# Four attention blocks on one core: the last block's key mask inside the key tile, its exps one PSUM bank at a time, another order of the merged stretch, and each bf16 term of its queries loaded behind its own store

## The reference

```python
def _L3_xattn_ref(x, mask, kv, kv_mask, Wq, bq, Wk, bk, Wv, bv):
    q = jnp.einsum('oc,bct->bot', Wq, x) + bq[None, :, None]
    k = jnp.einsum('oc,bct->bot', Wk, kv) + bk[None, :, None]
    v = jnp.einsum('oc,bct->bot', Wv, kv) + bv[None, :, None]
    ...
    attn = jnp.einsum('bhqd,bhdk->bhqk', q * scale, k)
    attn = jnp.where(kv_mask[:, :, None, :], attn, -jnp.inf)
    attn = jax.nn.softmax(attn, axis=-1)
    mean = jnp.einsum('bhqk,bhkd->bhqd', attn, v)
    ex2 = jnp.einsum('bhqk,bhkd->bhqd', attn, v * v)
    std = jnp.sqrt(jax.nn.relu(ex2 - mean * mean))
    ...
    out = (xn * std + mean) * mask.astype(x.dtype)
```

## Time and profile before

| | us |
|---|---|
| median of 3 runs | 1008.47 (1007.87 to 1010.12) |
| the profiled execution, its own time | 1012.25 |
| its span, first to last instruction | 1010.5 |
| PE busy | 935.5 (93%) |
| DVE busy | 559.5 (55%) |
| ACT busy | 456.2 (45%) |
| POOL busy | 292.4 (29%) |

### The profile page before, as it was taken

The page is one execution under the profiler, slowest core; times in us unless marked ns, Lnnn a source line. Parts: engine busy times, 40 slices in busy tenths (PEclk is TensorE's granted clock), DMA queues, the critical chain, the costliest instruction groups (busy, mean ns, idle before and its releaser), DMA issues.

```text
span 1010.5 us, 21161 instructions
## 1 busy us (share of the span) xinstructions
PE 935.5 (93%) x8450; PEld 596.5 (59%) x8450; DVE 559.5 (55%) x890; ACT 456.2 (45%) x795; POOL 292.4 (29%) x402
## 2 busy tenths in 40 slices
PE   6989989999999998999999999999999999898995
PEld 5555764666647665567646666466665675455552
DVE  4344467445664557555675456644576546664554
ACT  2423444445444544445544454345544454442424
POOL 5230222334212432115322242124321243222401
PEclk9999999999999999999999999999999999999999
DMA  9500324113140132303241130401414031310220
GB/s 362 190 38 2 125 75 146 38 43 136 36 156 19 57 139 81 108 6 126 79 146 38 43 134 32 154 28 43 141 50 143 14 120 44 119 53 2 98 55 6
DMA packets 36728, 86.54 MB, mean 86 GB/s; under 512 B 8472, under 2 KB 26008, under 8 KB 28824
## 3 DMA queue, kind: packets, MB, share of 16 engines
q1 hardware_dynamic: 36632, 85.18, 24.5%
HBM read 77.24 MB, written 7.86 MB: 84 GB/s over the span
## 4 chain that ended last, share of the span: by engine, by line
PE 67%; DVE 12%; issue 6%; DMA 5%; ACT 5%; SPq 4%; POOL 1%; DVEq 0%; ACTq 0%; POOLq 0%
PE GP L1107 6%; PE GP L1118 6%; PE GP L660 6%; DVE nm L1592 5%; PE GP L662 5%; PE PV L821 4%; PE GP L1091 4%; PE PV L860 3%; PE GP L900 3%; PE SC L883 3%; PE PV L1031 3%; DMA Qx<-q_parts 2%; PE GP L667 2%; PE SC L1018 2%; PE SC L804 2%
## 5 line engine op out<-in xcount | busy, mean ns | idle before, releaser
L1592 DVE TENSOR_REDUCE nm<-MX 128x4 bf16<-128x1024 f32 (+1 forms) x168 | 206.4, 1229 | 125.3 <-PE MX L751 48.3
L1363 ACT ACTIVATE Pr<-SC 128x1024 f32<-128x1024 f32 x120 | 122.7, 1023 | 153.6 <-PE SC L883 76.9
L1966 POOL TENSOR_TENSOR Psum<-Pr 128x512 f32<-128x512 f32 x64 | 81.5, 1274 | 163.4 <-ACT Pr L1363 163.4
L660 PE MATMUL GP<-zP,W 128*128 128x128 f32 x512 | 106.3, 290 | 7.7 <-DMA W<-w 7.7
L662 PE MATMUL GP<-uP,W 128*128 128x128 f32 x512 | 99.7, 277 | 0.0
L660 PEld LDWEIGHTS GP<-zP,W 128*128 128x128 f32 x512 | 78.3, 193 | 29.0 <-issue 27.3
L1392 ACT ACTIVATE Pr<-SC,bcol 128x512 f32<-128x512 f32 x96 | 60.8, 685 | 51.3 <-PE SC L1018 50.7
L1934 POOL TENSOR_TENSOR stat<-stat,half 128x1 f32<-128x1 f32 x24 | 13.7, 570 | 224.4 <-DVE stat L1800 171.2
L662 PEld LDWEIGHTS GP<-uP,W 128*128 128x128 f32 x512 | 78.5, 194 | 0.0
L821 PE MATMUL PV<-Pr,V 128*64 128x256 f32 x512 | 70.8, 398 | 0.0
L1118 PE MATMUL GP<-WB,work 128*128 128x256 f32 x256 | 60.8, 386 | 6.5 <-DVE work L1731 6.4
(11 more groups left out here) (221 smaller groups left out, 1750.3 us busy)
## 6 DMA issues: line engine op xcount, KB each, us to landing
W<-w SPq DMA_DIRECT2D x20, 1024.0 KB, 5.3
WA<-w1a SPq DMA_DIRECT2D x8, 1024.0 KB, 7.2
WB<-w1b SPq DMA_DIRECT2D x8, 1024.0 KB, 9.5
WA<-w2a SPq DMA_DIRECT2D x8, 1024.0 KB, 4.8
WB<-w2b SPq DMA_DIRECT2D x8, 1024.0 KB, 7.0
Kx<-k_parts SPq DMA_DIRECT2D x24, 192.0 KB
Qx<-q_parts SPq DMA_DIRECT2D x24, 192.0 KB
scratch<-U SPq DMA_DIRECT2D x14, 256.0 KB, 2.0
```

Of the source, the lines that this page charges most:

```text
L660: pe.matmul(dst, W0[:, piece, 2 * s, at:at + P], zP[:, s * P:s * P + P], start=True, stop=False)
L1363: act.activation(Pr[:, n % 4:n % 4 + 2, :], SCP[:], ACT.Exp, scale=8.0 ** -0.5 if L else 0.125)\
L1592: dve.tensor_reduce(dst, MXP[:].rearrange("p i (a k) -> p i a k", a=a), AX_X, ALU.max, negate=True)\
L1966: pool.tensor_tensor(Psum[:, c % 4, :].rearrange("p (a l) -> p a l", l=D), two[:, :, 0:D], two[:, :, D:2 * D], ALU.add)\
```

## The change

Four things. (1) The 128 mask matmuls (line 725) go. Each query block now carries a 1 in a row that no channel uses, and the mask row is added to the same row of `K3b`, by two DVE instructions per entry behind the third norm (`scalar_tensor_tensor`, 128 x 256). For this `Q3b` needs eight variants instead of four: DVE makes two, ACT six (all eight for the last entry); four lie in `Q3c`, a part of `work`. (2) Stage 3's exps go one bank at a time in every stretch. (3) `BOTH` has another order. (4) Each query term is stored and loaded by itself: the load of the high term stands right behind its store, ahead of the stores of the other two (not for the last entry), and waits for that store alone; its source repeats one term three times, as the keys' did, and the keys' loads take the form that the queries' had.

```diff
-        (0, 4, [(0, 3, 2), ("rest", 0)], [(3, 0, 0)]),
-        (0, 5, [("den", 1), ("terms", 0), (0, 3, "T"), ("recip", 0, 0)], [(3, 0, 2)]),
-        (0, 6, [], [("recip", 0, 1), (3, 1, 0)]), (0, 7, [(3, 0, "T"), (3, 1, 2)], [("den", 2), (3, 2, 0)]),
-        (3, 0, [], [(3, 2, 2), ("den", 3), (3, 1, "T")]), (3, 1, [(0, 0, "B")], [(3, 2, "T")]),
...
+        (0, 4, [("rest", 0), (0, 3, 2)], [("terms", 0)]), (0, 5, [(0, 3, "T")], [(3, 0, 0), ("den", 1)]),
+        (0, 6, [("recip", 0, 0), (3, 0, 2)], [("recip", 0, 1), (3, 1, 0), (3, 0, "T")]),
+        (0, 7, [(3, 1, 2)], [("den", 2), (0, 0, "B"), ("den", 3)]),
+        (3, 0, [("recip", 1, 0), (3, 2, 0), (3, 1, "T")], []), (3, 1, [(3, 2, 2)], []),
...
@@ key_terms, query_terms
-                store_terms(b, k_parts, (s_K3h, s_K3m, s_K3l), st_k)
+                store_terms(b, k_parts, ((0, s_K3h, st_k), (1, s_K3m, st_k), (2, s_K3l, st_k)))
...
-                    sp.dma_start(Kx[24 * j:24 * j + 24], k_parts[j:j + 1].to_broadcast([3, 8, NH * D]))\
-                        .then_inc(ld_kx, 16)
+                    sp.dma_start(Kx[24 * j:24 * j + 24], k_parts).then_inc(ld_kx, 16)
...
-                store_terms(b, q_parts, (s_Q3h, s_Q3m, s_Q3l), st_q)
-                sp.wait_ge(st_q, 48 * b + 48)
-                for j in range(3):
-                    sp.dma_start(Qx[24 * j:24 * j + 24], q_parts).then_inc(ld_qx, 16)
+                store_terms(b, q_parts, ((0, s_Q3h, st_q[0]),))
+                if not is_last(b):
+                    load_term(b, 0)
+                store_terms(b, q_parts, ((1, s_Q3m, st_q[1]), (2, s_Q3l, st_q[2])))
+                for i in range(3 if is_last(b) else 2):
+                    load_term(b, i if is_last(b) else i + 1)
+            def load_term(b, i):
+                sp.wait_ge(st_q[i], 16 * b + 16)
+                sp.dma_start(Qx[24 * i:24 * i + 24], q_parts[i:i + 1].to_broadcast([3, 8, NH * D])).then_inc(ld_qx, 16)
@@ maxima_pair3
-                    t = 2 * (g // 2) + u // 2
+                    v = 4 * (g // 2) + u + g % 2
...
-                    for i in range(2):
-                        half = slice(64 * i, 64 * i + 64)
-                        pe.matmul(M[i][:].rearrange("p (a k) -> p a k", k=D), sel[half, 0, :],
-                                  mrow[half, :].unsqueeze(1).to_broadcast([64, 2, D]), start=True, stop=False,
-                                  skip_group_check=True)
@@ scalar, mixed
-                    if is_last(b):
-                        exps_last(b, k)
+                    if L == 3:
+                        exps3(b, k)
...
-                    if b >= 0 and L == 0 and k == 4:
-                        queries3(b)
+                    if b >= 0 and L == 0 and k in (4, 5):
+                        queries3(b, (1, 3, 4) if k == 4 else (6, 5, 7))
@@ vector, behind layer_norm(b, xa, ..., 3)
+                dve.wait_ge(s_msk, N_MSK * b + 3)
+                dve.wait_ge(s_K3v, b + 1)
+                for e in range(2):
+                    ins = dve.scalar_tensor_tensor(out=K3b[:, e, :], in0=b3row[:], scalar=hmask[:, 14 + e:15 + e],
+                                                   in1=K3b[:, e, :], op0=ALU.mult, op1=ALU.add)
+                ins.then_inc(s_K3b, 1)
```

More of the change, by code:

```diff
@@ L249, in build @@
         Q3b = sb("Q3b", [P, 4, D], BF16)
+        Q3c = work[:, 1536:2048].bitcast(BF16).rearrange("p (v l) -> p v l", l=D)
         V0 = sb("V0", [P, 2, 1024])
@@ L331, in build @@
         ld_w0v = sem("ld_w0v")
-        st_k, st_q, ld_kx, ld_qx = sem("st_k"), sem("st_q"), sem("ld_kx"), sem("ld_qx")
+        st_k, ld_kx, ld_qx = sem("st_k"), sem("ld_kx"), sem("ld_qx")
+        st_q = [sem(f"st_q{i}") for i in range(3)]
         const_x = sem("const_x")
@@ L511, in shifts, with query3 @@
             return (s_T3, 4 * b + g + 1) if L == 3 else (nmT_ready, SHIFTS.index((b, L, g)) + 1)
+        def query3(v):
+            return Q3b[:, v, :] if v < 4 else Q3c[:, v - 4, :]
         def turned3(b, g):
@@ L581, in load_values, with store_terms @@
                 sp.dma_start(W0[:, 4], w0[4 + n % 2]).then_inc(ld_w0v, 16)
-            def store_terms(b, scr, ready, stored):
-                for i, s in enumerate(ready):
+            def load_term(b, i):
+                sp.wait_ge(st_q[i], 16 * b + 16)
+                sp.dma_start(Qx[24 * i:24 * i + 24], q_parts[i:i + 1].to_broadcast([3, 8, NH * D])).then_inc(ld_qx, 16)
+            def store_terms(b, scr, terms):
+                for i, s, stored in terms:
                     sp.wait_ge(s, b + 1)
@@ L683, in ready_group @@
                         pe.wait_ge(s_Q3b, b + 1)
[L684 to L685 removed]
+                    else:
+                        pe.wait_ge(s_Q3, 3 * b + g)
                     if g == 0:
@@ L730, in maxima_pair3 @@
                             half = slice(64 * i, 64 * i + 64)
-                            mm = pe.matmul(M[i][:, s * D:s * D + D], Q3b[half, t, s * P:s * P + P],
-                                           K3b[half, g % 2, :], start=False, stop=True, skip_group_check=True)
+                            mm = pe.matmul(M[i][:, s * D:s * D + D], query3(v)[half, s * P:s * P + P],
+                                           K3b[half, g % 2, :], start=True, stop=True, skip_group_check=True)
                             if s == 1:
@@ L1329, in highs3, with queries3, exps3 @@
                 act.activation(parts[:, 0, :], g[:, 0:D], ACT.Identity, bias=col("bq")).then_inc(s_Q3h, 1)
-            def queries3(b):
+            def queries3(b, which):
                 g = take(order_of(b), "q3")
                 act.wait_ge(s_Q3r, b + 1)
[L1335 to L1338, removed]
+                for v in which:
+                    ins = act.activation(query3(v), g[:, 0:D], ACT.Identity, scale=hmask[:, 4 + v:5 + v],
+                                         bias=col("bqm", v))
+                    if v == 2:
                         ins.then_inc(s_Q3b, 1)
-                ins.then_inc(s_Q3, 1)
-            def exps_last(b, k):
+                    elif v in (3, 6, 7):
+                        ins.then_inc(s_Q3, 1)
+            def exps3(b, k):
                 for j in range(2):
@@ L1354, in mixed @@
                     n = SC_AT[b + (L == 0), L, 2 * k]
-                    if is_last(b):
-                        exps_last(b, k)
+                    if L == 3:
+                        exps3(b, k)
                         if k == 4:
                             sums(b, 0)
+                        if k == 1 and b < B - 1:
+                            evacuate(b + 1, 3)
                         continue
@@ L1496, in keys3 @@
                     for e in range(2):
-                        ins = act.activation(K3b[:, e, :], g[:, 0:D], ACT.Identity, scale=hmask[:, 8 + e:9 + e],
+                        ins = act.activation(K3b[:, e, :], g[:, 0:D], ACT.Identity, scale=hmask[:, 12 + e:13 + e],
                                              bias=col("bkm", e))
-                    ins.then_inc(s_K3b, 1)
-                    wait(act, st_q, 48 * b)
+                    ins.then_inc(s_K3v, 1)
+                    wait(act, st_q[0], 16 * b)
                     act.activation(parts[:, 0, :], g[:, 0:D], ACT.Identity, bias=col("bk")).then_inc(s_K3h, 1)
@@ L1851, in body @@
                     dve.wait_ge(s_Q3h, b + 1)
-                    for t in range(2):
-                        ins = dve.tensor_scalar(Q3b[:, t, :], g[:, 0:D], col("bq"), hmask[:, 4 + t:5 + t],
-                                                ALU.add, ALU.mult)
+                    for v in (0, 2):
+                        ins = dve.tensor_scalar(query3(v), g[:, 0:D], hmask[:, 4 + v:5 + v], col("bqm", v),
+                                                ALU.mult, ALU.add)
                     ins.then_inc(s_Q3b, 1)
@@ L1972, in keys3 @@
                 pool.wait_ge(s_K3r, b + 1)
+                for stored in st_q[1:]:
+                    wait(pool, stored, 16 * b)
                 pool.tensor_copy(parts[:, 1, :], rest_k).then_inc(s_K3m, 1)
@@ L2096 @@
             at = slice(32 * r + 8 * t, 32 * r + 8 * t + 8)
-            bqm[t, at], bkm[r % 2, at] = bq[at], bk[at]
+            bqm[2 * t + r % 2, at], bkm[r % 2, at] = bq[at], bk[at]
+            if t < 2:
+                bqm[[v for v in range(8) if v % 2 != r % 2 and (v < 2) == t], 32 * r + 8 * t] = 1.0
     w0 = np.stack([a["L0_xattn_" + n].T for n in ("Wqkv0", "Winj0", "Wqkv1", "Winj1")], axis=1)
```

35 lines of the change are left out of this document (16 added, 19 removed), and 2 rows, old and new, of the table TAKEN.

## The result

The changed kernel takes 1052.3 us (median of 4 runs, 1049.23 to 1055.08) against 1008.9; the ratio is 1.0429 [1.039, 1.0468]. It is slower by 4.3%, outside the range forecast. The profiled execution took 1049.23 us, its span is 1047.4.

The account below looks back on a forecast made before the run. PE was taken as the bound (busy 93% of the span), DVE nearly as full in the first part. Stretches -8.4, queries' loads -2.5, last stretch +1.4: -9.5 us, giving a median of 999.0; range 986 to 1009.

Parts of the forecast that it names:

- The first part: From q3 to first scores3 in a merged stretch: DVE sets the pace, scores3 starts at 14.7 us, against 14.6 undisturbed before.
- The masks of the first part thus buy no time there: From q3 to first scores3: -0.2 us of PE work is given back as +0.3 of waits for DVE.
- The second part: From first scores3 to the projections: 17.3 us for 18.6; with the first part -1.2 a stretch, -8.4 in seven.
- The exps' -0.3 a stretch: Second part: two one-bank exps free the first bank half a microsecond sooner than a two-bank exp, -0.3 us per stretch.
- The queries' loads: Loads of the query terms ahead of scores3: all landed at 14.1 us from q3, 0.6 to spare before 14.7.
- one load of 196.6 KB in the new form takes 2.55 us: One query term's load on three DMA engines at 77 GB/s, the rate seen while the keys load in the repeating form.
- The last stretch: Three loads behind all stores land at 12.5 us, scores3 was at 10.7: +1.8, less 0.4 of masks, +1.4 us.
- The K3b instructions: Two DVE instructions of 0.48 us per entry behind the third norm: hidden in DVE's idle time; uncovered, 7.6 us.
- Rival (d): Three engines too few for the queries' loads: data end at 6.3 + 3d; d 3.6 gives +13 us, 1021.5; chance 0.12.
- The rule by which the forecast was to be judged wrong: PE's wait for the queries' load over the earlier 6.0 us by more than 2 would mean three engines bind.
- These rows don't show what delayed it there: The queries' load before the change, late in four of seven stretches by up to 1.7 us: cause left open.
- I take back -2.5: PE's waits for the queries' load outside the last stretch: 2.5 of 4.4 us regained, 0 to -4.8 kept possible.

Follow-up runs that it names:

- a_old_loads: The changed kernel with the queries' and keys' loads as before (all terms onto 24 rows, three times, behind all three stores): 993.82 us, ratio 0.986 to the kernel before.
- i_turned: The changed kernel with the repetition turned: each of a term's 8 rows repeated three times in place, slowest dimension 8, not 3; keys laid out to match: 993.49 us.
- g: The changed kernel with the high term's load behind all three stores, still repeating, weights issued behind the loads without waiting for them: 1055.34 us, ratio 1.0439 to before.
- c: The changed kernel, but SP waits until the queries' terms have landed before it issues the next entry's weights: 1028.04 us, ratio 1.0185 to the kernel before.
- h: The changed kernel with the high term's load behind all stores, and the weights issued only when the queries' terms have landed: 1014.4 us, ratio 1.0025 to before.
- p_masks: The kernel before with only the mask row in K3b and eight query variants (old order, exps and loads): 1003.14 us, ratio 0.9936 to the kernel before.
- f: The changed kernel with each term's load cut into three of eight rows, written three partitions apart, keys laid out to match: 996.97 us, ratio 0.9863 to before.

## Why the prediction was wrong

Forecast 999.0 us, measured 1052.3: 53 us off, on the other side of no change.

- **The first part** was right where the queries are there: PE was ready at 14.5 in the change and started at 14.44 in a_old_loads, for 14.7. Its reason was wrong in part. "The masks of the first part thus buy no time there" is refuted: they buy 0.8 to 0.9 us (14.58 to 13.64, 15.24 to 14.44), and the order costs 0.7 to 0.8.
- **The second part**: 17.3 forecast, 17.0 measured without the new loads. A stretch gains 14.58 + 18.6 - 31.44 = 1.74 us for the forecast 1.2; seven give -12.2 for -8.4. The exps' -0.3 a stretch was -0.2.
- **The queries' loads** are the step that failed: "Landed at **14.1**", where in the third stretch they landed at 20.4 and scores3 started at 20.7. The number of engines was right: the DMA share of 0.21 while the loads run alone is that of three. The Trainium skill (DMA: Bandwidth & Descriptors, "Why a DMA increments its semaphore by 16 and not by 1") has the slowest dimension set it; the trace agrees, also in i_turned, where 8 in that place doubles the share to 0.43 and mends the kernel. Sizes were wrong. First, "one load of 196.6 KB in the new form takes 2.55 us" was taken from a window without other traffic; beside the weights a packet takes 0.6 us, so the 16 packets that each engine carries for loads 1 and 2 need 9.6 us and not 5.1. Second, the first packets of a load take longer than the 0.31 us of the others, mostly 0.7 to 1.5 in the change's merged stretches; the sum had none of that. Third, the stores behind the high term's load were seen at 9.0, not 7.5. Moving them ahead is worth nothing while the weights move up with them (g), and 13.6 us when they don't (c to h). In the third stretch the data of loads 1 and 2 start at 10.5 for the forecast 8.9, and from there to the landing it is 9.9 us for 5.2; that is the whole 6.3 us from 14.1 to 20.4.
- **The clock** was in no term: after waits of 4.4 to 6.3 us TensorE ran at 1.2 GHz for a while, 13.1 us in all. Such a piece also followed the two longest waits in the merged stretches before the change, of 1.6 and 1.8 us; the second part took 19.8 there behind the first of them, for 18.6. None followed the waits of 1.7 to 2.6 in p_masks.
- **The last stretch**: 12.5 forecast, 13.76 measured. By the trace's packets the data start at 5.0 and end at 13.1, for the forecast 4.8 and 12.5, nearly all at 0.31 us a packet since no weights flow here; the other 0.6 us lie between the last packet and scores3.
- **The K3b instructions**: hidden, as forecast; 84.9 us stand between the stretches in all kernels.
- **Rival (d)** is what happened, by its own mechanism ("when stores and weights share these engines"), at a chance of 0.12 and a price too low: it took 3.6 us for a load beside the weights. By the packets of the third stretch that is what the high term's load took, ahead of the weights, and loads 1 and 2 took nearly 5 each. Its formula needs a d of 4.7 to give 6.3 + 14.1 = 20.4; that value is fitted, not found. The rule by which the forecast was to be judged wrong, over 2 us more of this wait, showed it: 43.8 for 6.0.
- **"These rows don't show what delayed it there"**, of the late load before: its third store. In the third stretch it was issued at 6.5 and landed 3.3 us later, for the 2.0 of the others (what held it isn't shown); issued at 5.1, as the new order has it, its loads were in time in all seven stretches of a_old_loads. "I take back -2.5" was worth -4.4.

The row set against the keys' window was no quiet one either. The window "while the queries load", 0.87 and 195 GB/s, ends at 520.05, and SP had issued the next entry's weights at 516.51. So that is the rate of the queries' loads with weights among them. In the last stretch, where no weights follow, the plain form alone moved 140 GB/s (the issue of the weights, then the window of the last stretch):

```profile
516.51 0.36 SPq L529 DMA_DIRECT2D WA<-w1a  x1
...
981.80:985.30 3.50, 3.09 (x22) 1.32 (x22) 3.06 (x3) 0.00 (x0) 0.00 (x0) 1.00 0.62 140
```

A load beside the weights was thus to be seen in the trace before the change; the sum took its rate from the keys' window, which has none.

Put together by the profiled spans: -12.2 in seven stretches, -4.4 of old waits, -1.7 in second parts that were longer than 18.6 before, -0.5 in the last stretch are -18.8, for 992.0 - 1010.5 = -18.5; the new loads add 55.4.

What stays open: why the first packets of a load take so long, and so differently (0.3 to 1.6 us); what it is in neighbouring rows that slows a load; and why all engines slow down when one of these loads runs beside the weights. i_turned changes the number of engines and the rows written at a time together; no run keeps three engines and changes the rows. None of these was tried further.

## What to carry to other kernels

A load's form decides how many DMA engines carry it. Before one that somebody waits for is moved earlier, ask what flows on the same engines by then, and price it from a window with that traffic, not from a quiet one. If a source must repeat, put the repetition inside, behind a dimension that gives more engines, and let one load reach partitions that lie apart. And a wait of several us on PE can cost more than its length, when what follows runs at the lower clock.

## What the runs showed of the hardware

- **The queries' loads and the weights slow each other down, in all four forms measured.** The weights alone move 416 to 419 GB/s with all 16 engines busy (a_old_loads at 13.0 to 15.5, c, f). Beside the queries' loads the engines are as busy, but move 217 GB/s with the old form, 248 with three engines, 232 with the turned one, and 143 with eight neighbouring rows. What sets the three-engine form apart is how long it lasts: at least 8 us in the change, some 2.5 in i_turned, where less of the loads is left when the weights come. A full DMA share is no sign of a full rate. Of a_old_loads, third stretch, loads beside weights, then weights alone; then of i_turned, loads beside weights:

```profile
393.09:397.09 4.00, 3.33 (x34) 1.66 (x29) 3.94 (x5) 2.00 (x3) 1.26 (x1) 1.00 0.94 217
397.69:400.19 2.50, 2.50 (x34) 0.93 (x26) 1.60 (x3) 0.63 (x2) 0.69 (x1) 1.00 1.00 416
...
396.40:398.80 2.40, 2.26 (x24) 1.12 (x24) 2.34 (x3) 1.02 (x1) 0.39 (x1) 1.00 1.00 232
```

- **A store's landing waits for a load ahead of it.** The second and third store took 4.4 and 4.0 us to land behind the three-engine load (issued at 4.53 and 5.13, landed at 8.95 and 9.14), 2.0 without it (g). That load's packets end at 8.4, and the stores' last ones stand right behind them, from 8.4 to 8.8.
- **An issue's length depends on its form**: by the timeline's rows, their length divided by their count, SP needs 0.38 us for each of the three plain loads of 24 rows, 0.75 to 0.81 for one that repeats in the outer place, 0.72 in the inner one, 0.65 for eight rows three apart, 0.33 for eight neighbouring ones.
